# Paged attention in a twelve-stage decoder: the loads of the first three stacks move past the stores of the projected queries and keys

## The reference

```python
def _L1_attn_ref(x, wq, w_down, wk_up, wv_up, wo):
    q = (x @ wq).reshape(B, T, H, D)
    lat = x @ w_down
    k = (lat @ wk_up).reshape(B, T, H, D)
    v = (lat @ wv_up).reshape(B, T, H, D)
    q = _apply_rope(q, cos, sin)
    k = _apply_rope(k, cos, sin)
    scores = jnp.einsum('bqhd,bkhd->bhqk', q, k) * scale
    pages = jnp.arange(T) // PAGE_SIZE
    allowed = pages[None, :] <= pages[:, None]
    scores = jnp.where(allowed[None, None], scores, jnp.finfo(scores.dtype).min)
    attn = jax.nn.softmax(scores, axis=-1)
    out = jnp.einsum('bhqk,bkhd->bqhd', attn, v).reshape(B, T, E)
    return out @ wo
```

## Time and profile before

| what | value |
|---|---|
| median of 3 runs | 2747.84 us (2745.88 to 2752.18) |
| the profiled execution | 2748.86 us, its span 2747.1 us |
| TensorE busy | 2432.6 us, 89% of the span |
| VectorE, ScalarE, GpSimd busy | 1438.9, 946.2 and 494.6 us |
| DMA | 181.47 MB, mean 66 GB/s |
| projection part of the paged attention | about 499 to 578 us from the span's start |
| its score part | from 578 us |

### The profile page before, as it was taken

How to read it: one execution, slowest core, us unless ns; L and a number is a source line. 1 busy time by engine, 2 the same in 40 slices (tenths; PEclk the granted TensorE clock), 3 DMA queues, 4 the chain that set the end, 5 groups by cost and what they waited for, 6 DMA issues and landing times. The chain is left out here.

```text
span 2747.1 us, 36310 instructions
## 1 busy us (share of the span) xinstructions
PE 2432.6 (89%) x14259; PEld 1686.0 (61%) x14259; DVE 1438.9 (52%) x2474; ACT 946.2 (34%) x1799; POOL 494.6 (18%) x422
## 2 busy tenths in 40 slices
PE   6986767778889879979999998889999799999888
PEld 3665654422224768856667667757776577777764
DVE  7996979367773421036564653651110455455543
ACT  3443657225554213234442431311111322122132
POOL 3442320220001124310100011122221311001010
PEclk8998989969999979999999999779999899999999
DMA  3003100373420046622322230322231300000000
GB/s 113 1 1 122 48 32 1 58 145 50 69 44 26 5 173 226 226 89 89 93 71 65 67 98 0 104 58 101 77 90 56 103 18 18 12 18 12 1 33 31
DMA packets 77659, 181.47 MB, mean 66 GB/s; under 512 B 16935, under 2 KB 41128, under 8 KB 71945
## 3 DMA queue, kind: packets, MB, share of 16 engines
q1 hardware_dynamic: 64596, 126.74, 16.7%
q0 software_dynamic: 10368, 50.01, 5.3%
q10 hardware_dynamic: 2542, 2.62, 0.3%
HBM read 149.51 MB, written 25.43 MB: 64 GB/s over the span
## 5 line engine op out<-in xcount | busy, mean ns | idle before, releaser
L1655 PE MATMUL L_ffn_h_ps<-L_ffn_xgT,L_ffn_w 128*128 128x512 f32 (+2 forms) x992 | 231.9, 390 | 4.0 <-DVE L_ffn_xgT L1738 2.3
L1667 PE MATMUL L_ffn_y_ps<-L_ffn_w,L_ffn_h 128*128 128x256 f32 x1008 | 222.5, 380 | 4.8 <-issue 3.9
L1713 ACT ACTIVATE L_ffn_h<-L_ffn_h_ps,L_ffn_w 128x640 f32<-128x640 f32 (+2 forms) x184 | 101.6, 553 | 346.1 <-PE L_ffn_h_ps L1655 335.0
L527 DVE TENSOR_REDUCE L_attn_neg<-L_attn_Y 128x1 f32<-128x512 f32 (+3 forms) x304 | 187.4, 657 | 55.8 <-PE L_attn_Y L400 54.4
L1667 PEld LDWEIGHTS L_ffn_y_ps<-L_ffn_w,L_ffn_h 128*128 128x128 f32 x1008 | 189.9, 190 | 32.9 <-issue 8.3
L1655 PEld LDWEIGHTS L_ffn_h_ps<-L_ffn_xgT,L_ffn_w 128*128 128x128 f32 x992 | 153.8, 192 | 81.5 <-issue 66.8
L497 ACT ACTIVATE L_attn_room<-L_attn_Y 128x1024 f32<-128x1024 f32 (+1 forms) x192 | 147.4, 812 | 81.1 <-PE L_attn_Y L451 80.5
L400 PE MATMUL L_attn_Y<-L_attn_K,L_attn_Q 104*128 104x512 bf16 (+3 forms) x384 | 119.6, 363 | 44.9 <-DVE L_attn_neg L527 35.9
L1747 DVE TENSOR_TENSOR L_ffn_yg<-L_ffn_y_ps,L_ffn_w 128x256 f32<-128x256 f32 x63 | 26.7, 425 | 223.5 <-PE L_ffn_y_ps L1667 223.5
L1738 DVE COPY L_ffn_xgT<-L_ffn_t_ps 128x256 f32<-128x256 f32 x63 | 24.5, 421 | 212.1 <-PE L_ffn_t_ps L1642 211.7
L1788 POOL DMA_INDIRECT token_outputs<-L_ffn_yg,puts x63 | 61.8, 982 | 324.5 <-DVE L_ffn_yg L1747 324.5
(11 more groups left out here) (577 smaller groups left out, 5099.3 us busy)
## 6 DMA issues: line engine op xcount, KB each, us to landing
L_ffn_w<-in_L_ffn_w SPq DMA_DIRECT2D x8, 2180.0 KB
L_attn_bc<-decays SPq DMA_DIRECT2D x32, 512.0 KB, 6.1
L_attn_bp<-decays SPq DMA_DIRECT2D x32, 256.0 KB, 7.0
L_attn_Q<-L_attn_q_parts SPq DMA_DIRECT2D x48, 128.0 KB, 4.7
L_attn_K<-L_attn_k_parts SPq DMA_DIRECT2D x48, 128.0 KB, 7.6
L_attn_first_w<-in_L_attn_w SPq DMA_DIRECT2D x8, 640.0 KB
L_attn_w<-in_L_attn_w SPq DMA_DIRECT2D x8, 640.0 KB, 3.8
L_attn_v_all<-zero SPq DMA_DIRECT2D x1, 4096.0 KB, 22.5
```

The lines of the kernel that those rows point to most:

```text
L527: nc.vector.tensor_reduce(neg[:, c, j0:j0 + heads, tt], R[n % 2][:, 0:heads * width(tt, c)].rearrange("p (h k) -> p h k", h=heads), X_AXIS ...
L1655: ins = nc.tensor.matmul(h_ps[f % 2][:, lo // CW, 0:hi - lo], w1[g % NB][:, kt, f * P:(f + 1) * P], xgT[u][:, kt, lo:hi], start=kt == 0, s ...
L1667: ins = nc.tensor.matmul(y_ps[k % 2][:], h[:, f, t * P:(t + 1) * P], w2[g % NB][:, f, :], start=f == 0, stop=f == FT - 1)
L1713: nc.scalar.activation(h[:, f, 0:n], h_ps[f % 2][:].rearrange("p c n -> p (c n)")[:, 0:n], func, bias=b1[g % NB][:, f:f + 1]).then_inc(sem ...
```

## The change

The loads of the first three stacks are taken from behind the stores of rounds 2 and 3 of the first half and put ahead of the stores of rounds 0, 1 and 2 of the second half, one each. The waits before them are the same.

```diff
             for b in range(B):
                 for r in range(NR):
-
+                    if b == 1 and r < SLOTS:
+                        sp.wait_ge(stored[r // 2], 16 * NR)
+                        load(sp, r)
                     sp.wait_ge(part_done[2], b * NR + r + 1)
                     for g in range(2):
                         it = b * NG + r % 2 * 2 + g
                         sp.dma_start(parts_dram[r // 2][:, it:it + 1, :, :].rearrange("c i p t -> p (c i) t"),
                                      parts[g * G * DH:(g + 1) * G * DH, r % 2, :, :]).then_inc(stored[r % 2], 16)
-                    if b == 0 and r >= 2:
-                        for slot in range(2 * r - 4, min(2 * r - 2, SLOTS)):
-                            sp.wait_ge(stored[slot // 2], 16 * NR)
-                            load(sp, slot)
```

## The result

The changed kernel took 2748.29 us (median of 20 runs, 2734.18 to 2753.11), and the kernel before, run beside it, 2754.71 (20 runs, 2745.25 to 2763.87). The ratio is 0.9974 with a 95% interval of 0.9961 to 0.9986: 0.26% or some 7 us less, between 4 and 11. The forecast was 7.6 us less. The time itself, 2748.29, lies above the forecast 2740.2 and above its range, which ended at 2745.5. The difference came out as forecast; the level did not, since the kernel before, whose three runs had a median of 2747.84, has one of 2754.71 over twenty. Two executions in the experiments further down, at 3856 and 8333 us, were far slower than all others and enter no ratio.

The account below looks back on a forecast made before the run. The prediction took the late store of round 3, first half, holding up ScalarE's cast and so VectorE's maxima, as the bound. Its one gain, 7.6 us with other terms at nothing, gave 2747.84 - 7.6 = 2740.2 us, range 2736 to 2745.5.

Parts of the forecast that it names:

- What bounds the stage: Second half: late store of round 3, first half, delays ScalarE's cast of round 1, VectorE's round 3 and the maxima.
- The store of round 3: First half, SP's list: issued at 541.6 ahead of all loads, lands about 547; VectorE's round 3 starts 7.6 us earlier.
- The loads: First stack lands 557.4, wanted 562.82; second about 575; both cost nothing, with 5.5 us of issuing for a stack.
- The cast of round 3: Second half: ScalarE's cast waits for the store of round 1 until about 575.5; nobody on the path but SP waits.
- The bound of 0 to 5 us for this place: DMA engines' queued traffic ahead of the first scores: a loss of 0 to 5 us possible, taken as 0.
- The clock: TensorE's idle time before the first scores is 7.5 us shorter; no difference in time was taken for it.
- rival 2: TensorE's clock comes back earlier, first scores run at 2.4 GHz: 2 to 2.5 us more gain, 2738; chance 0.08.
- Rival 4: Slower: second-half loads delay round 1's store, then line 378 and first scores; 2754 at 30 us a stack; chance 0.03.
- The skill's fit: DMA engines: 2.0 us plus bytes over 436 GB/s gives 5.6 us for a stack, making the loss there nil.
- The sum: Whole program: 7.6 us off the median 2747.84 gives 2740.2 us, 0.28% less.
- All later stages move as a whole.: Everything behind the maxima comes earlier together, since nothing there is tied to a clock time.
- a sign of being wrong: First scores at 603.6 while the end of the stage does not move with them would show the prediction wrong.

Follow-up runs that it names:

- only the third stack moves: Against the kernel before, only the third stack's load moved, ahead of the second half's round 2 store; ratio to before 0.9994.
- one stack stays: Changed kernel, but stack 0's load stays between the stores of rounds 2 and 3 of the first half; ratio to before 0.9958.
- all between: Changed kernel, but all three stacks' loads stand between the last store of the first half and the first of the second; ratio to before 0.9973.
- the store on ScalarE's queue: Kernel before, no load moved, with the first half's round 3 store issued by ScalarE instead of SP; ratio to before 0.9981.
- the third buffer: Changed kernel plus another buffer for rotated rows, used by round 3 of each half; ratio to before 0.9930, again 0.9948.

## Why the prediction was right and where it was wrong

- **What bounds the stage.** Right: the chain from the store through cast, subtraction, VectorE's round 3 and the maxima. One part of it undone (only the third stack moves) takes the gain away, and other ways to let the store land in time (one stack stays, all between, the store on ScalarE's queue) start the maxima as early.
- **The store of round 3.** Expected landing about 547, measured 542.1 + 5.0 = 547.1. Cast of round 1 at 559.9 expected, 559.72 measured; VectorE's round 3 at 566.5, measured 566.34; maxima at 570.1, measured 569.94. The term was 7.6 us and measured 7.8; of the 0.2 between them 0.16 is that the stage began earlier in the second profile (509.07 against 509.23).
- **The loads.** The first two were costed at nothing, rightly. Their issuing was mis-sized: 5.5 us for a stack (called half of 11.4, which is 5.7), measured 4.97 + 3.02 = 8.0 behind a store (542.7 to 550.8) and 8.9 for the second stack (558.92 to 567.8). That used up the margin ahead of the store of round 1, which was issued at 567.83 and not 566.4. No price followed.
- **The cast of round 3.** 575.5 expected, 574.54 measured; SP free at 592, measured 591.1. Line 376 in time, with 8.4 us to spare. The bound of 0 to 5 us for this place was real: the run with the store on ScalarE's queue paid 2.6.
- **The clock.** It was back at 2.4 GHz about 3 us after the first scores instead of 5.6 (by the granted clock at 606.4, and at 616.8 before). The values' first matmuls are 8.4 us earlier instead of 7.8, 0.6 us in the direction of rival 2. This isn't shown to be the change's: in the second profile of before the clock was back 3.5 us after the first scores, too, and the values' first matmuls came 5.1 us after them as in the changed kernel (5.65 in the first).
- **Rival 4.** By its own terms a stack of 30 us gives a cast at 559.0 + 30 + 4 = 593, line 378 some 16.5 us later at 609.5 and a time near 2750, not 2754. It did not happen.
- **The skill's fit.** The prediction sets 5.6 us for a stack, by the Trainium skill ("DMA: Bandwidth & Descriptors", Anatomy of one DMA), beside the row's 12.5. The page gives that fit for DMAs issued from GpSimd, and these are SP's. The sum did not use it.
- **The sum.** Difference 7.6 us forecast; by the ratio 4 to 11 us measured, by the pieces 7.8 up to the first scores. Direction and size of the difference were right. What failed is the step from the difference to the time: "the median to expect is 2747.84 - 7.6", with "the scatter of a median of few runs adds about 1.5 us on each side". Twenty runs of before, of which the three shown were the first, spread from 2745 to 2764 with a median of 2754.71, so the three lay 6.9 us low. Three later sets of before (35, 17 and 29 runs) have medians of 2751.9, 2751.0 and 2751.8, so a median of twenty is itself good to some 3 us only. Applied to 2754.71 the same difference gives 2747.1, and 2748.29 was measured. The profiles had a warning that I took for a detail: their spans hold pieces of 1880 us that no line of the change touches.
- **"All later stages move as a whole."** The first pair of profiles doesn't bear this out, and the prediction had named it as a sign of being wrong: the first scores came at 603.43 and the last ones moved by 2.2 us only. Over ten profiles the score part takes back 1.4 us in the mean, and the pieces behind it scatter by more than the gain. So the step is wrong by a part of the 7.8 us that the runs bound only roughly; the ratio (4 to 11 us) says that half of the gain or more is kept.

What stays open is how much of the 3 us taken back half-way through the score part lasts to its end, since its length differs by 6.7 us among the thirteen profiles, and why the clock falls where it does.

## What to carry to other kernels

A store in a queue's list is waited for by whoever reuses its buffer, often a round later and on another engine, so it belongs ahead of loads that nobody wants yet; what matters is that it lands before its buffer is wanted, and here nothing more was gained by landing earlier. After such a move the next thing to read is what the queue has to issue last before the next phase asks for it, since the phase now asks earlier. And a small difference is forecast as a difference: the level of three runs can lie further off than the gain.

## What the runs showed of the hardware

- A store behind 24 loads in one queue landed in 12.4, 14.4 or 16.5 us (medians of three profiles), behind 12 loads in 8.2, and alone in 4.4. SP issued the store behind 24 loads at 552.2 to 552.4 each time, so the scatter is not SP's. The Trainium skill ("DMA: Bandwidth & Descriptors", Queues, rings and completion order) says that descriptors of one ring are taken in their order; these landing times agree with it.
- Issuing a stack of twelve loads took SP 5.5 us before the change (540.76 to 546.30), where the last store had been issued 4 us earlier, and 8.0 right behind one (542.7 to 550.8), where the longest single issue took 1.6 us.
- Behind the gap between the halves, eight matmuls took 3.70 us after 3.54 us of idling in all three profiles with the third buffer (granted clock 1.00 in 533 to 537), and 6.7 us after 5.93 in the other ten (0.56 in 532 to 539 of the changed kernel), 3.0 us more.
- The same program's execution scatters by 0.7% (2745 to 2764 us), in pieces all over the program. Within the score part short stretches at 1.2 GHz come near the ends of items, at different items in different executions; the two early ones stand in all six profiles with 94.4 us to the first scores.
- VectorE's third rotary step of round 3 (128 x 1024, f32) took 1.23 us in the changed kernel and 2.99 with the third buffer, where it ran beside a subtraction of GpSimd (564.60 to 566.72); the same step of round 2 took 1.99 beside one in the changed kernel (562.05, GpSimd 560.84 to 562.97).
